# Message steps of six and five gather groups in turn, with 24 groups behind the last step

## The chip, the cores and the metric

The kernel runs on one core of one Trainium2 chip. The metric is the device time of one execution in microseconds. The kernel before took 2603.88 us, the median of 3 runs (2602.32 to 2604.92).

The engines are called TensorE (PE in the profile; PEld is its weight load, PEldq its sequencer's own instructions), VectorE (DVE), ScalarE (ACT), GpSimd (POOL) and SyncE (SP).

## The reference

`x` has 12500 rows (nodes) of 256 floats. `src` and `dst` name 200000 edges, sorted by `dst`; low node numbers have many more edges than high ones. What is computed:

```python
xn  = layernorm(x)
agg = segment_sum(xn[src], dst) / max(count of edges per dst, 1)
gnn = relu(agg @ W_l.T + b_l + xn @ W_r.T) + xn
# linear attention over all 12500 rows, 8 heads of 32:
Q, K = elu(xn @ Wq) + 1, elu(xn @ Wk) + 1;   v = xn @ Wv
msg  = (Q @ sum(K v)) / (Q . sum(K) + eps);  msg = layernorm(msg @ Wm) * g1 + b1
msg  = layernorm(relu(concat(xn, msg) @ W1) @ W2) * g2 + b2
x = x + gnn + (xn + msg)
# then: layernorm of x, a score per row, the 6249 best rows go through a
# gelu MLP of width 1024, are scaled by their score and added to x
```

## The kernel before, in words

Rows are tiled in 98 blocks of 128, two blocks to a step, so there are `NSUP` = 49 steps. The phases follow each other:

1. Normalization. The normalized rows go to a table in HBM (`xtab`) as two fp16 halves, high and low part, 512 fp16 values a row.
2. Key steps (49): K, Q and v of two blocks, sums over all rows, and Q and the transposed rows written to HBM.
3. Message steps (49): attention message, its projection, a two-layer MLP, and the product with `W_r`. A step is `m_body` on TensorE, VectorE and ScalarE, and `m_io` on SyncE. Two steps are unrolled in a loop body, `s` being the parity and `j` the number of the pair.
4. Linear phase: means of the aggregate (ScalarE, L1422, its first instruction waits for `agg_done`), their product with `W_l` (L1722) and the stored product of `W_r`, which GpSimd loads again (`lin_raw`, L722).
5. Choice of the best rows, and their MLP.

Along phases 2 and 3 runs the aggregation. The edges are cut into `NG` = 392 groups of 512, each of 4 lists of 128. GpSimd takes them in order (L708): per list one indirect DMA gathers 128 rows of `xtab` into a ring of `RING` = 6 slots (group g in slot g % 6). Before the first gather of group g it waits until group g - 6 is used (`grp_used`), and each gather raises the arrival semaphore `rows_in[slot]` by 16. The last five lists are left out, so group 390 has three gathers and group 391 none.

VectorE makes for every group and every block of nodes that the group touches a one-hot matrix (`one_hot`, L880), in 4 buffers. TensorE's `seg` (L1540 and on) loops over the blocks of a group: it waits for the arrival semaphore, the one-hot and a zeroed PSUM bank, multiplies each list twice (high part L1550, low part and count L1552), and after the last block marks the group as used (L1561). When a block is complete, VectorE adds its sum to `agg` and zeroes the bank (`add_before`, L890 and L892).

The groups are written into the steps by hand. A key step has 2 (groups 0 to 97). A message step has 6 in steps 0 to 41 and 5 in steps 42 to 48; 7 follow behind the last step, between the leftovers of it (`m_hidden`, `l_product`, `m_mlp_out` on TensorE, `norm_stats` and `m_end` on VectorE). With six groups a step the slot is the place in the step, so all slots are numbers of the program text. After the last group VectorE calls `add_before` twice, then reads the counts and sets `agg_done`.

What sets the order of the work is this text: each engine takes its instructions in order, and semaphores tie them.

Of the kernel before, what the change touches and what calls it, by code (L numbers as in the profile page):

```python
# [9 lines left out]
ALU = mybir.AluOpType  # L10
# [3 lines left out]
P = 128  # L14
N, D, E = 12500, 256, 200000
# [5 lines left out]
TPG = 4  # L21
GE = TPG * P
KG, MG = 2, 6
NG = NSUP * (KG + MG)
RING = 6
TAIL = 7
MFULL = NSUP - TAIL
# [35 lines left out]
assert NSUP % GCH == 0 and 0 < LASTC < P and KG * 3 == RING and MG == RING and MFULL % 2 == 0  # L63
# [52 lines left out]
def build(nc, x, src, dst, W_l, b_l, W_r, Wq, Wk, Wv, Wm, W1, W2, g1, b1, g2, b2, wr, br, w1, fb1, w2, fb2, out):  # L116
# [13 lines left out]
    with ctx:  # L130
# [147 lines left out]
        ones_set = sem("ones_set")  # L278
# [4 lines left out]
        k_x_in = [sem(f"k_x_in{i}") for i in range(3)]  # L283
# [17 lines left out]
        m_x_in = [sem(f"m_x_in{i}") for i in range(2)]  # L301
# [44 lines left out]
        s_in_col = sem("s_in_col")  # L346
        s_lane = sem("s_lane")
        s_a = sem("s_a")
# [120 lines left out]
        def k_place(s, j, t):  # L469

            return KG * s + t, j

        def m_first(i):

            return KG * NSUP + MG * i - (max(0, i - MFULL) if isinstance(i, int) else 0)

        def m_groups(i):

            return MG - 1 if isinstance(i, int) and i >= MFULL else MG

        def place(g):

            return g % RING, g // RING

        def m_place(i, t):

            if isinstance(i, int):
                return place(m_first(i) + t)
            slot, use = place(KG * NSUP + t)
            return slot, use + i  # L490

        tail = list(range(NG - TAIL, NG))

# [24 lines left out]
        def _(e):  # L518
# [43 lines left out]
            for i in range(2):  # L562
                e.dma_start(kx[i], rows(x, 2 * i)).then_inc(k_x_in[i], 16)
# [6 lines left out]
            def k_io(i, s, j):  # L570
                if not (isinstance(i, int) and i >= NSUP - 2):
                    if past(i, 1):
                        e.wait_ge(k_xn, i)
                    e.dma_start(kx[(s + 2) % 3], rows(x, 2 * i + 4)).then_inc(k_x_in[(s + 2) % 3], 16)
# [11 lines left out]
            def m_load(i, s):  # L586
                e.dma_start(mx[s], rows(x, 2 * i)).then_inc(m_x_in[s], 16)
                e.dma_start(flat(mq[s]), turned(q_d, i)).then_inc(m_q_in[s], 16)
# [70 lines left out]
        def _(e):  # L659
# [38 lines left out]
            e.memset(gath[:, :, 2 * D:2 * D + 1], 1.0).then_inc(ones_set, 1)  # L698
# [66 lines left out]
        def _(e):  # L765
# [222 lines left out]
            def m_body(i, s, j):  # L988
                g0 = m_first(i)
                spans = seg_values(e, mybir.EngineType.DVE, g0, m_groups(i))  # L990
# [35 lines left out]
                for t in range(5, m_groups(i)):  # L1026
# [6 lines left out]
            for t, g in enumerate(tail):  # L1033
                seg(g, BA, *seg_values(e, mybir.EngineType.DVE, g, 1)[0])
# [16 lines left out]
            add_before()  # L1051
            k = e.snap(full)
            e.wait_ge(seg_added, k + 2)
# [149 lines left out]
            for c in range(NPCH):  # L1203
                k, b = c % 2, slice(c * PCH, (c + 1) * PCH)
                if c >= 2:
                    e.wait_ge(s_mm, c - 1)
                v.tensor_tensor(s_is[k], bcast(col16, PCH, NSEL), s_col[:, b].unsqueeze(2).to_broadcast([P, PCH, NSEL]),
                                ALU.is_equal).then_inc(s_in_col, 1)
                v.tensor_tensor(s_oh[k], bcast(iota16, PCH, P), s_pos[:, b].unsqueeze(2).to_broadcast([P, PCH, P]),
                                ALU.is_equal)  # L1210
                e.wait_ge(s_in_col, c + 1)
                v.tensor_tensor(s_pc[k][:, :, NSEL:2 * NSEL], s_is[k], blk16[:, b].unsqueeze(2).to_broadcast([P, PCH, NSEL]),
                                ALU.mult).then_inc(s_a, 1)
# [55 lines left out]
        def _(e):  # L1269
# [52 lines left out]
            e.wait_ge(k_x_in[0], 16)  # L1322
# [4 lines left out]
            def k_body(i, s, j):  # L1327
                more = not (isinstance(i, int) and i == NSUP - 1)
                s1 = (s + 1) % 3
                if more:  # L1330
                    e.wait_ge(k_x_in[s1], 16 * (j + (s + 1) // 3) + 16)
                    e.wait_ge(k_xT_ps, i + 1)
                    xn_of(kxn, kx[s1], i + 1, k_xn)
# [53 lines left out]
            def m_body(i, s, j):  # L1387
# [13 lines left out]
                e.wait_ge(m_x_in[s], 16 * j + 16)  # L1401
# [64 lines left out]
            for c in range(NPCH):  # L1466
                e.wait_ge(s_in_col, c + 1)
# [37 lines left out]
        def _(e):  # L1505
# [32 lines left out]
            def seg(slot, use, first, more, end):  # L1538

                padded = max(0, (use * RING + slot + 1) * TPG - (NG * TPG - GPAD)) if isinstance(use, int) else 0  # L1540
                landed = 16 * TPG * use + 16 * (TPG - min(TPG, padded))
# [17 lines left out]
                one = gath[:, TPG * slot, 2 * D:2 * D + 1]  # L1559
# [5 lines left out]
            e.wait_ge(ones_set, 1)  # L1565

            e.wait_ge(agg_zero, NBATCH)
# [18 lines left out]
            def k_body(i, s, j):  # L1586
# [14 lines left out]
                seg(*k_place(s, j, 0), *spans[0])  # L1601
# [10 lines left out]
                seg(*k_place(s, j, 1), *spans[1])  # L1612
# [37 lines left out]

            def m_body(i, s, j):
# [10 lines left out]
                g0 = m_first(i)  # L1662
                spans = seg_values(e, mybir.EngineType.PE, g0, 1)
                seg(*m_place(i, 0), *spans[0])
                if past(i, 1):
                    m_hidden(i - 1, 1 - s, j - 1 + s, 0)
                spans += seg_values(e, mybir.EngineType.PE, g0 + 1, m_groups(i) - 1)
                seg(*m_place(i, 1), *spans[1])
# [4 lines left out]
                seg(*m_place(i, 2), *spans[2])  # L1673
# [8 lines left out]
                seg(*m_place(i, 3), *spans[3])  # L1682
                if past(i, 1):
                    m_mlp_out(i - 1)
                seg(*m_place(i, 4), *spans[4])
                e.wait_ge(m_yn, i + 1)
                transposes(BB, myn).then_inc(m_yT_ps, 1)
                for k in range(5, m_groups(i)):
                    seg(*m_place(i, k), *spans[k])
            steps(e, m_body, MFULL, 2)  # L1690
            for i in range(MFULL, NSUP):
                m_body(i, i % 2, i // 2)

            i = NSUP - 1
            for k, g in enumerate(tail):
                seg(*place(g), *seg_values(e, mybir.EngineType.PE, g, 1)[0])
# [5 lines left out]
                if k == 2:  # L1702
                    m_mlp_out(i)

# [52 lines left out]
            for c in range(NPCH):  # L1757
                e.wait_ge(s_a, c + 1)
# [82 lines left out]
```

## Time and profile before

| | us |
|---|---|
| median of 3 runs | 2603.88 |
| profiled execution | 2605.66 |
| its span, first to last instruction | 2603.9 |
| TensorE matmul busy | 2193.5 (84%) |
| GpSimd busy | 1695.5 (65%) |
| VectorE busy | 1329.9 (51%) |
| ScalarE busy | 901.4 (35%) |

Shares of the chain that ended last: TensorE 45%, GpSimd 29%, issue 13%, VectorE 7%, DMA 5%. Its largest line is the gather L708 with 28%. Key steps lie between about 112 and 597 us, message steps between 597 and 2041 us, and the leftovers up to 2078 us.

A row of a wait table gives the engine and line that stood idle, what ended the idle time, the sum, the number of times and the longest. "issue" is time in which the engine waited for nothing that the profile shows. The ends of matmuls are modelled, so the time between two starts says more than the duration of one.

### The profile page before, as it was taken

To read this page: it belongs to the slowest core of one execution; us is meant where nothing else is said; L and a number is where in the kernel's file an instruction comes from. 1 tells how busy PE (TensorE), PEld (TensorE's weight loads), DVE (VectorE), ACT (ScalarE), POOL (GpSimd) and SP (SyncE) were. 2 spreads that over 40 slices of the span, in tenths; PEclk is the share of its full clock that TensorE was granted. 3 is DMA by queue.
4 is the path that set the end of the run, shared out by engine and by line. 5 is a ranking of instruction groups with operands and counts; after the bars stand their busy time and mean duration, and the time that the engine had idled before them with its cause. 6 is when DMAs were issued, how large, how long until landed. Compare 5 with 4: busy or idle time off the path is not lost.

```text
span 2603.9 us, 48868 instructions
## 1 busy us (share of the span) xinstructions
PE 2193.5 (84%) x13352; PEld 1818.9 (70%) x13353; DVE 1329.9 (51%) x3157; ACT 901.4 (35%) x1949; POOL 1695.5 (65%) x1817
## 2 busy tenths in 40 slices
PE   1399999997888888888888888988899799379998
PEld 0287777775667666666676666777677688279998
DVE  8644444443444344454444454455555599844444
ACT  8433333331222222222222222222222268344554
POOL 3577777777777777777777777777777411045553
PEclk7699999998898999999999999999999899589999
DMA  9766666654555555555555555555555489611111
GB/s 326 232 194 186 184 184 179 188 181 146 160 157 153 152 154 164 157 160 155 153 158 160 153 161 157 152 153 165 158 162 166 142 276 297 214 34 43 45 44 35
DMA packets 218373, 419.29 MB, mean 161 GB/s; under 512 B 40580, under 2 KB 107142, under 8 KB 218287
## 3 DMA queue, kind: packets, MB, share of 16 engines
q0 software_dynamic: 88352, 243.57, 33.0%
q1 hardware_dynamic: 129118, 173.95, 19.9%
q8 instruction: 34, 0.56, 0.1%
q10 hardware_dynamic: 816, 0.79, 0.1%
q14 instruction: 53, 0.43, 0.1%
HBM read 321.63 MB, written 96.52 MB: 161 GB/s over the span
## 4 chain that ended last, share of the span: by engine, by line
PE 45%; POOL 29%; issue 13%; DVE 7%; DMA 5%; ACT 1%; DVEq 1%; POOLq 0%; ACTq 0%
POOL gath_raw L708 28%; PE ps L1782 11%; PE ps L1629 6%; PE ps L1550 5%; PE ps L1552 4%; PE ps L1595 4%; DMA gath_raw<-xtab,srcI 3%; PE ps L1722 3%; PE ps L1639 3%; PE ps L1535 2%; PE ps L1677 2%; PE ps L1647 1%; DVE stats L784 1%; PE ps L1609 1%; DVE gath_raw L803 1%
## 5 line engine op out<-in xcount | busy, mean ns | idle before, releaser
L708 POOL DMA_INDIRECT gath_raw<-xtab,srcI x1563 | 1483.6, 949 | 476.5 <-issue 460.7
L1550 PE MATMUL ps<-gath_raw,onehot 128*128 128x256 f16 x1956 | 480.3, 283 | 202.8 <-DMA gath_raw<-xtab,srcI 107.6
L880 DVE SCALAR_TENSOR_TENSOR onehot<-ps,blkbase,dstF 128x512 f32 x489 | 353.9, 745 | 257.8 <-issue 154.5
L1552 PE MATMUL ps<-gath_raw,onehot 128*128 128x257 f16 x1956 | 481.5, 283 | 0.0
L1550 PEld LDWEIGHTS ps<-gath_raw,onehot 128*128 x1956 | 195.2, 100 | 292.9 <-issue 263.4
L1629 PE MATMUL ps<-work,w_s 128*128 128x256 f32 x1568 | 392.9, 407 | 2.2 <-issue 1.7
L1629 PEld LDWEIGHTS ps<-work,w_s 128*128 128x128 f32 x1568 | 311.7, 204 | 48.7 <-issue 2.7
L954 DVE BATCH_NORM_STATS2 stats<-ps 128x6 f32<-128x256 f32 x196 | 74.4, 421 | 449.2 <-PE ps L1677 444.6
L1782 PE MATMUL ps<-split_raw 128*128 128x256 f32 x2376 | 293.3, 285 | 1.7 <-DVE split_raw L1231 1.5
L1782 PEld LDWEIGHTS ps<-split_raw 128*128 128x128 f32 x2376 | 288.4, 193 | 2.4 <-issue 1.9
L1363 ACT ACTIVATE work<-ps 128x512 f32<-128x512 f32 x98 | 58.5, 597 | 496.8 <-PE ps L1629 496.8
L1552 PEld LDWEIGHTS ps<-gath_raw,onehot 128*128 x1956 | 197.2, 101 | 40.3
L1595 PE MATMUL ps<-wkv_s,work 128*128 128x256 f32 x784 | 183.1, 387 | 5.4 <-issue 4.7
L1639 PE MATMUL ps<-w_s,work 128*128 128x256 f32 x784 | 182.3, 385 | 0.0
L1595 PEld LDWEIGHTS ps<-wkv_s,work 128*128 128x128 f32 x784 | 146.1, 191 | 25.3 <-issue 5.4
L1639 PEld LDWEIGHTS ps<-w_s,work 128*128 128x128 f32 x784 | 144.9, 190 | 18.5
L1398 ACT ACTIVATE work<-ps,b_s,g_s 128x256 f32<-128x256 f32 x98 | 49.9, 560 | 247.3 <-PE ps L1535 247.3
L1368 ACT ACTIVATE small<-small 128x2 f32<-128x2 f32 x98 | 19.9, 203 | 329.6 <-DVE small L962 329.6
L1495 ACT ACTIVATE agg<-ps,fb_s 128x256 f32<-128x256 f32 x200 | 83.9, 470 | 138.4 <-PE ps L1782 138.4
L1535 PE MATMUL ps<-ident,work 128*128 128x128 f32 x784 | 124.6, 282 | 5.6 <-ACT work L1422 5.6
L722 POOL DMA_DIRECT2D lin_raw<-lin_d x49 | 26.0, 532 | 124.6 <-PE ps L1722 109.0
L1535 PEld LDWEIGHTS ps<-ident,work 128*128 128x128 f32 x784 | 91.1, 142 | 17.8 <-ACT work L1422 5.7
(223 smaller groups left out, 2989.9 us busy)
## 6 DMA issues: line engine op xcount, KB each, us to landing
work<-x_in SPq DMA_DIRECT2D x98, 256.0 KB, 3.2
lin_raw<-lin_d POOLq DMA_DIRECT2D x49, 512.0 KB, 4.4
gath_raw<-xtab,srcI POOLq DMA_INDIRECT x1563
agg<-x_in SPq DMA_DIRECT2D x14, 896.0 KB, 7.4
xt_d<-work SPq DMA_DIRECT2D x49, 256.0 KB
q_d<-work SPq DMA_DIRECT2D x49, 256.0 KB, 2.7
work<-q_d SPq DMA_DIRECT2D x49, 256.0 KB, 3.4
work<-xt_d SPq DMA_DIRECT2D x49, 256.0 KB, 3.1
```

Of the source, the lines that this page charges most:

```text
L708: e.indirect_dma_start(out=gath[:, TPG * s + t, 0:2 * D], out_offset=None, in_=xtab[:, :], in_offset=bass.IndirectOffsetOnAxis(ap=srcI[:, ...
L880: v.scalar_tensor_tensor(out=onehots[:, ds(p % OHN * TPG, TPG), :], in0=ps[:, columns:columns + 1, 0:P].to_broadcast(shape), scalar=blkbas ...
L954: last = v.bn_stats(ln_st[k][:, u, :], src[:, u, :])
L1495: last = a.activation(fh[:, c, :], bank(BB + h)[:, c % 2, :], ACT.Gelu_apprx_tanh, bias=fb1_s[:, c:c + 1])
L1535: last = t.transpose(bank(b)[:, c, u * P:(u + 1) * P], of[:, u, c * P:(c + 1) * P], ident[:, :])
L1550: t.matmul(ps[:, ds(BG + k % 2, 1), 0:D], oh, gath[:, r, 0:D], start=False, stop=False, skip_group_check=True)
L1552: last = t.matmul(ps[:, ds(BG + k % 2, 1), 0:AGW], oh, gath[:, r, D:2 * D + 1], start=False, stop=q == TPG - 1, skip_group_check=True)
L1595: last = t.matmul(bank(BC + b)[:, u, :], kxT[s][:, c, u * P:(u + 1) * P], wkv_s[:, c, b * D:(b + 1) * D], start=c == 0, stop=c == 1)
L1629: last = t.matmul(bank(BD + h)[:, o_ % 2, :], w1_s[:, c, o_ * P:(o_ + 1) * P], (mxT[s] if c < 2 else mynT)[:, c % 2, :], start=c == 0, sto ...
L1639: last = t.matmul(bank(BF)[:, u, :], mh1[:, c, u * P:(u + 1) * P], w2_s[:, c, :], start=c == 0, stop=c == 3)
L1722: last = t.matmul(to[:, u, :], gaT[i % 2][:, c, u * P:(u + 1) * P], wlT[:, c, :], start=False, stop=c == 1, skip_group_check=True)
L1782: last = t.matmul(to, left[l], right[r], start=start and k == 0, stop=stop and k == 2)
```

## The change

- Message steps have 6 groups where the step number is even and 5 where it is odd, in all 49 steps, and all of them run in the loop of pairs. That makes 270 groups. The remaining 24 follow the last step: the first six between its leftovers, the others in loops of six.
- A pair has 11 groups, so a place in the pair meets another slot each time. `seg` on TensorE takes the slot as a register value in the message steps, and its gather operand's row is computed from it.
- Arrival semaphores: `landing(g)` names the semaphore for group g. Within the message steps places 6 to 10 of a pair have five new ones (`rows_m`), everything else uses `rows_in[g % RING]`. GpSimd calls it with its g; TensorE's `m_seg` calls it with the group of the first pair at that place and adds `TPG * j` lists to the count.
- The group mark takes its operand from slot 0.
- After the last group VectorE adds the block before last ahead of the wait for the last mark, and the last block behind it, without zeroing a bank.
- Some semaphores are merged: `x_rows_in` for the loads of x in both kinds of steps, `agg_zero` for the ones of the ring, `s_placed` in the choice of rows.

```diff
-KG, MG = 2, 6
-NG = NSUP * (KG + MG)
+KG = 2
+MPAIR = (6, 5)
+NG = NSUP * 8
 RING = 6
-TAIL = 7
-MFULL = NSUP - TAIL
+MAT = KG * NSUP
+TAILAT = MAT + sum(MPAIR[i % 2] for i in range(NSUP))
+TAIL = NG - TAILAT
...
+        rows_m = [sem(f"rows_m{i}") for i in range(sum(MPAIR) - RING)]
...
+        def m_first(s, j):
+            return MAT + sum(MPAIR) * j + sum(MPAIR[:s])
+
+        def landing(g):
+            p = (g - MAT) % sum(MPAIR)
+            return rows_m[p - RING] if MAT <= g < TAILAT and p >= RING else rows_in[g % RING]
+
+        def landed(g):
+            return TPG * len([o for o in range(g + 1) if landing(o) is landing(g)])
...
-                    ).then_inc(rows_in[s], 16)
+                    ).then_inc(landing(g), 16)
...
-            e.wait_ge(grp_used, NG)
             add_before()
-            e.reg_mov(before, held)
-            e.reg_mov(since, pair)
-            add_before()
-            k = e.snap(full)
-            e.wait_ge(seg_added, k + 2)
+            e.wait_ge(grp_used, NG)
+            b, k = e.snap(held), e.snap(full)
+            v.tensor_tensor(agg[:, ds(b, 1), :], agg[:, ds(b, 1), :], ps[:, ds(BG + k % 2, 1), 0:AGW], ALU.add).then_inc(sum_read, 1)
+            e.wait_ge(sum_read, k + 1)
...
-            def seg(slot, use, first, more, end):
+            def seg(rows_of, lists, slot, first, more, end):
...
+                row = slot * TPG if isinstance(slot, int) else e.snap(slot * TPG)
+                landed_at = 16 * lists
...
-                    e.wait_ge(rows_in[slot], landed)
+                    e.wait_ge(rows_of, landed_at)
...
-                        r = TPG * slot + q
+                        r = row + q if isinstance(row, int) else ds(row + q, 1)
...
+            def m_seg(s, j, t, span):
+                g = m_first(s, 0) + t
+                seg(landing(g), landed(g) + TPG * j, (m_first(s, j) + t) % RING, *span)
...
-            steps(e, m_body, MFULL, 2)
-            for i in range(MFULL, NSUP):
-                m_body(i, i % 2, i // 2)
+            steps(e, m_body, NSUP, 2)
...
+            with e.Fori(1, TAIL // RING - 1) as j:
+                spans = seg_values(e, mybir.EngineType.PE, TAILAT + RING * j, RING)
+                for k in range(RING):
+                    seg(landing(TAILAT + k), landed(TAILAT + k) + TPG * j, (TAILAT + k) % RING, *spans[k])
```

## Rows read from the trace of the kernel before

**Rows 1.** The page's first line.
```profile
span 2603.9 us, 48868 instructions
```

**Rows 2.** GpSimd's waits, 130 to 2060 us: us in total, times, longest us.
```profile
POOL gath_raw L708 <- issue: 452.8, 1486, 0.3
POOL gath_raw L708 <- PE ps L1561: 15.5, 51, 0.3
```

**Rows 3.** Line L708, 900 to 1900 us: ns min/median/max, first and last start.
```profile
L708 POOL DMA_INDIRECT gath_raw<-xtab,srcI x799: 942/946/1416, 899.6 to 1899.9; - x200
```

**Rows 4.** Timeline of GpSimd, the last gather: start us, us, what, idle before.
```profile
2055.22 0.95 POOL L708 DMA_INDIRECT gath_raw<-xtab,srcI  x1 [0.30 <-issue]
```

**Rows 5.** Chain of waits, 2070 to 2080 us: start us, us, what.
```profile
2070.14 1.58 issue
2071.72 0.39 PE ps L1550
...
2073.61 0.11 PE ps L1561
...
2074.60 0.43 DVE agg L890
...
2076.36 0.43 DVE agg L890
...
2076.82 0.44 DVE ps L892
...
2078.36 0.92 ACT work L1422 x2
```

**Rows 6.** Stretches, line L1550 alone: length, PE busy (x), PEld (x), clock, DMA, GB/s.
```profile
597.00:1858.00 1261.00, 323.68 (x1296) 130.79 (x1296) 0.94 0.52 156
1858.00:2041.00 183.00, 48.42 (x209) 20.28 (x209) 1.00 0.54 162
```

**Rows 7.** Timeline of TensorE, step 46: its start, five marks, the next step.
```profile
1962.82 1.14 PE L1659 MATMUL ps<-kvk,work 128*128 128x132 f32 x8 [1.16 <-issue]
...
1966.76 0.16 PE L1561 MATMUL ps<-gath_raw 128*1 128x1 f16 x1
...
1971.60 0.16 PE L1561 MATMUL ps<-gath_raw 128*1 128x1 f16 x1
...
1977.55 0.16 PE L1561 MATMUL ps<-gath_raw 128*1 128x1 f16 x1
...
1982.18 0.16 PE L1561 MATMUL ps<-gath_raw 128*1 128x1 f16 x1
...
1986.81 0.16 PE L1561 MATMUL ps<-gath_raw 128*1 128x1 f16 x1
...
1988.72 1.14 PE L1659 MATMUL ps<-kvk,work 128*128 128x132 f32 x8 [1.16 <-issue]
```

**Rows 8.** Timeline of TensorE, fifth and sixth mark of step 36.
```profile
1702.53 0.16 PE L1561 MATMUL ps<-gath_raw 128*1 128x1 f16 x1
...
1704.93 0.16 PE L1561 MATMUL ps<-gath_raw 128*1 128x1 f16 x1
```

**Rows 9.** Chain of waits, 284 to 292 us; the first is a group's last gather.
```profile
286.02 2.97 DMA gath_raw<-xtab,srcI
288.99 0.52 issue
...
289.79 0.11 PE ps L1552
...
290.56 0.09 PE ps L1561
```

**Rows 10.** Chain of waits, 745 to 765 us: both halves of the hidden layer.
```profile
748.02 4.86 PE ps L1629 x16
...
754.20 3.65 PE ps L1629 x16
```

**Rows 11.** Line L1550, 1858 to 2041 us: register operations of TensorE's sequencer.
```profile
L1550 PEldq FUSED_REGOPS  x265: 46/46/143, 1859.3 to 2040.7; - x133
```

More of the change, by code:

```diff
@@ L282, in build @@
         bnd_tab = sem("bnd_tab")
-        k_x_in = [sem(f"k_x_in{i}") for i in range(3)]
+        x_rows_in = [sem(f"x_rows_in{i}") for i in range(3)]
         k_xn = sem("k_xn")
@@ L562, in _ @@
             for i in range(2):
-                e.dma_start(kx[i], rows(x, 2 * i)).then_inc(k_x_in[i], 16)
+                e.dma_start(kx[i], rows(x, 2 * i)).then_inc(x_rows_in[i], 16)
             e.wait_ge(bnd_out, 16)
@@ L573, in k_io @@
                         e.wait_ge(k_xn, i)
-                    e.dma_start(kx[(s + 2) % 3], rows(x, 2 * i + 4)).then_inc(k_x_in[(s + 2) % 3], 16)
+                    e.dma_start(kx[(s + 2) % 3], rows(x, 2 * i + 4)).then_inc(x_rows_in[(s + 2) % 3], 16)
                 e.wait_ge(k_xnT, i + 1)
@@ L586, in m_load @@
             def m_load(i, s):
-                e.dma_start(mx[s], rows(x, 2 * i)).then_inc(m_x_in[s], 16)
+                e.dma_start(mx[s], rows(x, 2 * i)).then_inc(x_rows_in[s], 16)
                 e.dma_start(flat(mq[s]), turned(q_d, i)).then_inc(m_q_in[s], 16)
@@ L1025, in m_body @@
                     l_even(i - 1, 1 - s, j - 1 + s)
-                for t in range(5, m_groups(i)):
+                for t in range(5, MPAIR[s]):
                     seg(g0 + t, BA, *spans[t])
-            steps(e, m_body, MFULL, 2)
-            for i in range(MFULL, NSUP):
-                m_body(i, i % 2, i // 2)
+            steps(e, m_body, NSUP, 2)
             last_two = [(i, own_m + 10 * NSUP - 10 + 5 * k) for k, i in enumerate((NSUP - 2, NSUP - 1))]
-            for t, g in enumerate(tail):
-                seg(g, BA, *seg_values(e, mybir.EngineType.DVE, g, 1)[0])
+            for t in range(RING):
+                seg(TAILAT + t, BA, *seg_values(e, mybir.EngineType.DVE, TAILAT + t, 1)[0])
                 if t in (0, 5):
@@ L1045, in _ @@
                     m_end(i, i % 2, ch + 3)
-            e.wait_ge(grp_used, NG)
-            add_before()
-            e.reg_mov(before, held)
-            e.reg_mov(since, pair)
-            add_before()
-            k = e.snap(full)
-            e.wait_ge(seg_added, k + 2)
+            with e.Fori(1, TAIL // RING) as j:
+                g0 = TAILAT + RING * j
+                spans = seg_values(e, mybir.EngineType.DVE, g0, RING)
+                for t in range(RING):
+                    seg(g0 + t, BA, *spans[t])
+            add_before()
+            e.wait_ge(grp_used, NG)
+            b, k = e.snap(held), e.snap(full)
+            v.tensor_tensor(agg[:, ds(b, 1), :], agg[:, ds(b, 1), :], ps[:, ds(BG + k % 2, 1), 0:AGW], ALU.add).then_inc(sum_read, 1)
+            e.wait_ge(sum_read, k + 1)
             base = own_m + 10 * NSUP
@@ L1400, in m_body @@
                 last.then_inc(m_ynT, 1)
-                e.wait_ge(m_x_in[s], 16 * j + 16)
+                e.wait_ge(x_rows_in[s], 16 * (len(range(s, NSUP, 3)) + j + 1))
                 if past(i, 2):
@@ L1466, in _ @@
             for c in range(NPCH):
-                e.wait_ge(s_in_col, c + 1)
+                e.wait_ge(s_placed, 2 * c + 1)
                 if c >= 2:
@@ L1558, in seg @@
                 e.reg_alu(full, behind, 0, op=ALU.max)
-                one = gath[:, TPG * slot, 2 * D:2 * D + 1]
+                one = gath[:, 0, 2 * D:2 * D + 1]
                 k = e.snap(full)
@@ L1600, in k_body @@
                 spans = seg_values(e, mybir.EngineType.PE, KG * i, KG)
-                seg(*k_place(s, j, 0), *spans[0])
+                seg(rows_in[KG * s + 0], TPG * (j + 1), KG * s + 0, *spans[0])
                 if more:
@@ L1611, in k_body @@
                 last.then_inc(k_q_ps, 1)
-                seg(*k_place(s, j, 1), *spans[1])
+                seg(rows_in[KG * s + 1], TPG * (j + 1), KG * s + 1, *spans[1])
             steps(e, k_body, NSUP, 3)
@@ L1681, in m_body @@
                     l_product(i - 1, 1 - s)
-                seg(*m_place(i, 3), *spans[3])
+                m_seg(s, j, 3, spans[3])
                 if past(i, 1):
                     m_mlp_out(i - 1)
-                seg(*m_place(i, 4), *spans[4])
+                m_seg(s, j, 4, spans[4])
                 e.wait_ge(m_yn, i + 1)
                 transposes(BB, myn).then_inc(m_yT_ps, 1)
[L1688 to L1692, printed above, removed]
+                for k in range(5, MPAIR[s]):
+                    m_seg(s, j, k, spans[k])
+            steps(e, m_body, NSUP, 2)
             i = NSUP - 1
-            for k, g in enumerate(tail):
-                seg(*place(g), *seg_values(e, mybir.EngineType.PE, g, 1)[0])
+            for k in range(RING):
+                seg(landing(TAILAT + k), landed(TAILAT + k), (TAILAT + k) % RING, *seg_values(e, mybir.EngineType.PE, TAILAT + k, 1)[0])
                 if k < 2:
@@ L1703, in _ @@
                     m_mlp_out(i)
+            with e.Fori(1, TAIL // RING - 1) as j:
+                spans = seg_values(e, mybir.EngineType.PE, TAILAT + RING * j, RING)
+                for k in range(RING):
+                    seg(landing(TAILAT + k), landed(TAILAT + k) + TPG * j, (TAILAT + k) % RING, *spans[k])
+            spans = seg_values(e, mybir.EngineType.PE, NG - RING, RING)
+            for k in range(RING):
+                missing = min(TPG, max(0, TPG * (k + 1) - (TPG * RING - GPAD)))
+                seg(landing(NG - RING + k), landed(NG - RING + k) - missing, (TAILAT + k) % RING, *spans[k])
             def g_turn(i):
```

54 lines of the change are left out of this document (17 added, 37 removed).

## The prediction, made before the result was known

> **What bounds the kernel now.** I read the span first, then GpSimd's waits, because its gathers (L708) head the chain. From 130 to 2060 us GpSimd never idled longer than 0.3 us before a gather, whoever released it [rows 2]. It issues one gather per 1.25 us: 799 start between 899.6 and 1899.9 us, so (1899.9 - 899.6) / 798 = 1.2535, and 1.25 in stretches without a 1416 ns one [rows 3]. A group of four takes 5.01 us. So the 392 groups are bound by GpSimd's issue, and the last gather starts at 2055.22 us [rows 4]. Nothing TensorE does better can move that; what can move it is a slot that comes free late.
>
> The second view is TensorE over the message steps. The gap from the last gather's start to the first use of the means, at 2078.36, is 23.14 us [rows 4, 5]: TensorE is several groups behind at the end. A step of five groups that waits for no gather takes 1988.72 - 1962.82 = 25.90 us with 7 one-hot blocks [rows 7], against 25.03 us of gathers, so the last seven steps lose ground. After its last group mark a five-group step needs 1.91 us to the next step [rows 7]; a sixth group, one block, comes 2.40 us after the fifth mark [rows 8] and about 0.13 more ends the step: 25.90 - 1.91 + 2.53 = 26.52 us.
>
> **The new order of steps.** 49 steps hold 25 x 6 + 24 x 5 = 270 groups, and 24 follow. A pair of steps costs TensorE 25.90 + 26.52 = 52.42 us at 7 + 8 blocks. Blocks are fp16 matmuls of L1550 over four: 1296 / 4 = 324 in 252 groups early, 209 / 4 = 52 in 35 groups late [rows 6], so 14.1 and 16.4 per 11 groups. At 8 starts 0.11 us apart [rows 9], 0.88 us each, the pair is 51.6 and 53.7 us. GpSimd needs 44 x 1.2515 = 55.06. By this alone GpSimd stays the bound and TensorE arrives at the tail hardly behind. The tail's 24 groups take 120 us of gathers, far more than TensorE's leftovers of the last step (about 13 us of matmuls) plus some 2 us a group.
>
> **The end of the aggregation, shorter.** Now only the two last groups stand behind the last gather (group 391 has none). A seg starts 2.97 + 0.52 = 3.49 us after the last gather of its group starts [rows 9]. In a tail half idle I expect the lower clock level, as at the end of this one, where a block with its mark takes 2073.72 - 2071.72 = 2.0 us [rows 5], against 290.65 - 289.51 = 1.14 in the stretch of rows 9; two, with 0.5 between (bounds 0.1 and the 1.58 of a row in which the bounds are loaded between), give 3.49 + 2.0 + 0.5 + 2.0 = 8.0. From mark to sum is 2074.60 - 2073.72 = 0.9; then 2078.36 - 2076.36 = 2.0, less 0.45 for the zeroing no longer there [rows 5]. In all 10.4 us against 23.14: 12.7 saved, between 11 and 15 (full clock). The second add now costs nothing, since its first half stands ahead of the wait. The lin loads of GpSimd, which today wait for the last store behind the last gather, start at once, but were not the last wait before either. What is late next is the landing of the last gather. The phases behind begin as before and shift whole.
>
> **The waits, a cost that the title hides.** The scatter matmuls wait on landing(g). GpSimd evaluates it with the real g: for the first six places of a pair that is rows_in[g % 6]. TensorE evaluates it with the g of the first pair plus TPG * j. A pair has 11 groups, and 11 mod 6 is 5, so in pair j the semaphore on which place p waits is the one that the group at place (p + j) mod 6 increments. The five other places are exact. Hence, at j mod 6 = 1, place 4 has waited for place 5's group; at 2, place 0 waits for place 2's; and so on; at j mod 6 = 5, place 0 waits until the group five later has landed. Each gather of that group may start, as slots are free up to it; the next group's may not, since its slot is the one place 0 holds. At j mod 6 = 0 all is exact. Where the place waited for is an earlier one nothing is held.
>
> For j mod 6 from 1 to 4 this only makes TensorE trail by one to four groups; it has the slots for it. At j = 5, 11, 17, 23 GpSimd stops. With S the start of the last gather of the group waited for, the next gather was due at S + 1.25; place 0's mark ends at 290.65 - 286.02 = 4.63 after S [rows 9], so it stands 3.4 us, up to 3.7 with the issue gap of 0.3 [rows 2]. Then, marks in a step that waits for no gather: 4.84, 10.79, 15.42, 20.05 us after the first [rows 7], against 5.01, 10.01, 15.02, 20.02: the third is 0.8 late. So 4.3 us per event at full clock. But TensorE has just idled 5 us or more; after such gaps the 16 matmuls of L1629 took 4.86 us in place of 3.65 [rows 10], and a block 2.0 in place of 1.14: +0.9 and +1.2 or twice that. That makes 6.4 to 7.6. At j mod 6 = 4 (places 0 and 1 wait for places 4 and 5) the third mark comes at S + 4.63 + 10.79 = 15.4 against 1.25 + 15.02 = 16.3 due: nothing at full clock, 1 to 3 us at half clock or with a two-block first group. Per round of six pairs 4.3 to 11 us; I take 7, nearest to the half-clock rows. Four rounds: 28 us, between 17 and 44. TensorE regains 1.4 to 3.4 us of lag per pair between events, which is why the stop comes again in full each time: every j mod 6 = 5 demands five groups of lag exactly.
>
> The Trainium skill (DMA: Bandwidth & Descriptors, Anatomy of one DMA, SWDGE path) fits a GpSimd DMA of 128 KB at 2.0 + 0.3 = 2.3 us. The trace has 2.97 from the instruction's start, 2.02 from its end. Were 2.3 counted from the end, each stop and the last landing would be 0.3 longer: 1 us more in the sum.
>
> **Registers for the slot.** Gather slices in the message steps get their row from a register. Per block the sequencer runs 265 / 52 = 5 fused register operations of 46 ns [rows 6, 11], and matmuls start 0.11 us apart all the same [rows 9]. Cost bounds: nothing, or one more for each of 8 matmuls, 0.37 us x 14.1 = 5.2 us a pair, making 51.6 into 56.8, 1.8 over GpSimd, x 24.5 pairs = 43 us. I take nothing, the nearer row: the array works off 0.22 us per one-hot quarter, and one operation more hides there. The remainder by six, once per group, is hidden the same way, up to a few tenths after a wait.
>
> The merged semaphores (x_rows_in, agg_zero, s_placed) keep each wait at the same event: nothing, either way, as no instruction is added. Fewer unrolled steps: nothing seen, below 1 us.
>
> **Sum.** The profiled execution is 2605.66 us (span 2603.9 [rows 1] plus 1.8 around it). 2605.66 - 12.7 + 28 = 2621; its own time stood 1.8 above the median of the three runs, so 2619.
>
> **Rivals.** First, the other side: the later-place waits never stop GpSimd, because TensorE is that late anyway or the count is satisfied by other arrivals; then only the end gains: 2603.9 - 12.7 = 2591. It would decide if TensorE trailed five groups without being asked; against it stands that today it waits for gathers, that is, it trails by one group. Chance 0.17. Second, register arithmetic makes TensorE the bound: 2591 + 43 = 2634, and with part of the stops on top, 2634 to 2650. For it: a sequencer that must do twice as much between matmuls; against: the unchanged matmul spacing. 0.13. Third, the change does not do what it says but cheaply: stops at full clock and no more, 17 us, cancel the end's gain: 2591 + 17 = 2608, no measurable change. For it: clock 0.94 in the message steps [rows 6], so mostly full. 0.12. The forecast, 2619, own range 2609 to 2634, has 0.58.
>
> The range reaches from the first rival to the second's upper part: 2590 to 2647. Something like 0.2% (5 us) is what a measurement tells from no change: faster 0.18, same 0.11, slower 0.71.
>
> **What would show it.** GpSimd's waits: today's longest before a gather is 0.3 us; I expect four stops of 3.4 us or more near groups 159, 225, 291 and 357, with shorter ones up to 2 groups around, and 28 us in sum. TensorE's waits for gathers at place 0 of the six-group steps should be 5 us and more for j mod 6 = 1 to 5 and absent at 0. The last gather should start near 2083 us, and 10 us later the first use of the means. The step pairs should run at 55 us. Matmul spacing in L1550's group should stay 0.11; if it grows, the second rival. If the last gather still starts at 2055, the first rival is right and my reading of landing is wrong.

## The result, and the profile after

The changed kernel takes 2747.2 us (2745.89 to 2754.93, five runs) against 2603.88 us (2602.32 to 2606.46) for the kernel before: ratio 1.0557, 95% interval 1.0542 to 1.0572. That is 143 us slower, where 15 us were predicted; it lies outside the range. In 13 of the 18 runs of the next section the kernel before took 3062 to 3096 us instead of 2604 to 2606, for a cause that was not found; they are called the 3080 us runs below, the others the 2604 us runs, and every ratio is taken within one of the two groups.

First the page of the changed kernel: the span, then busy time and share of each engine.

```profile
span 2750.5 us, 51654 instructions
...
PE 2267.9 (82%) x13352; PEld 1837.3 (67%) x13353; DVE 1331.1 (48%) x3156; ACT 901.9 (33%) x1949; POOL 1696.1 (62%) x1817
```

The span stands against 2603.9 in [rows 1]. GpSimd's busy time is what it was (1695.5), TensorE's grew by 74 us. GpSimd's waits before a gather come next (us in total, times, longest us, 130 to 2210 us); they answer to [rows 2]:

```profile
POOL gath_raw L696 <- issue: 437.5, 1409, 1.4
POOL gath_raw L696 <- PE ps L1551: 187.8, 125, 8.1
```

The second line is the result in one row. GpSimd's wait for a free slot (the mark of TensorE, L1551) was 15.5 us with none above 0.3; now it is 187.8 us with a longest of 8.1. GpSimd no longer bounds the message steps. The last gather shows the sum (timeline: start, us, what, idle before); it answers to [rows 4], 2055.22:

```profile
2212.93 0.95 POOL L696 DMA_INDIRECT gath_raw<-xtab,srcI  x1 [0.30 <-issue]
```

So the gathers end 157.7 us later. The end of the aggregation, in the chain of waits (start, us, what), answers to [rows 5]:

```profile
2209.18 2.75 DMA gath_raw<-xtab,srcI
2211.93 0.52 issue
2212.45 0.39 PE ps L1540
...
2216.14 0.27 issue
2216.41 0.39 PE ps L1540
...
2219.18 0.12 PE ps L1551
...
2219.99 0.44 DVE agg L1042
...
2221.53 0.92 ACT work L1412 x2
```

From the last gather's start to the first use of the means it is 2221.53 - 2212.93 = 8.6 us instead of 23.14: 14.5 us less. And 157.7 - 14.5 = 143.2 us, all but 3.4 of the 146.6 us between the two spans. The gain at the end came about as predicted; the loss is in the message steps.

### The profile page after: what moved, and what is told of

It reads as the page before. It is cut to its first block, busy times and chain, and to the rows that moved or that the text cites. A ratio compares the mean times of both kernels' runs of the same rounds, so it can differ in the third digit from the quotient of the medians.

```text
span 2750.5 us, 51654 instructions
## 1 busy us (share of the span) xinstructions
PE 2267.9 (82%) x13352; PEld 1837.3 (67%) x13353; DVE 1331.1 (48%) x3156; ACT 901.9 (33%) x1949; POOL 1696.1 (62%) x1817
## 4 chain that ended last, share of the span: by engine, by line
PE 60%; issue 13%; POOL 10%; DVE 9%; DVEq 4%; DMA 3%; ACT 1%; POOLq 0%; ACTq 0%; SPq 0%
PE ps L1618 13%; PE ps L1782 10%; POOL gath_raw L696 9%; PE ps L1540 8%; PE ps L1542 6%; PE ps L1584 4%; PE ps L1628 4%; PE ps L1671 3%; PE ps L1722 3%; DVEq L463 2%; PE ps L1525 2%; DMA gath_raw<-xtab,srcI 2%; PE ps L1636 2%; DVE onehot L868 1%; PE ps L1551 1%
## 5 line engine op out<-in xcount | busy, mean ns | idle before, releaser
L1540 PE MATMUL ps<-gath_raw,onehot 128*128 (+1 forms) x1956 | 505.4, 288 | 236.7 <-DVE onehot L868 126.8
L868 DVE SCALAR_TENSOR_TENSOR onehot<-ps,blkbase,dstF 128x512 f32 x489 | 355.4, 746 | 439.6 <-issue 373.4
L1542 PE MATMUL ps<-gath_raw,onehot 128*128 (+1 forms) x1956 | 510.3, 290 | 0.0
L1540 PEld LDWEIGHTS ps<-gath_raw,onehot 128*128 x1956 | 194.4, 99 | 352.9 <-issue 290.0
L1618 PE MATMUL ps<-work,w_s 128*128 128x256 f32 x1568 | 403.6, 415 | 6.2 <-issue 4.5
L1618 PEld LDWEIGHTS ps<-work,w_s 128*128 128x128 f32 x1568 | 319.2, 209 | 57.9 <-issue 6.8
L1551 PEld LDWEIGHTS ps<-gath_raw 128*1 128x1 f16 x392 | 31.0, 79 | 118.9 <-issue 118.9
```

Source lines behind the costliest of these rows:

```text
L868: v.scalar_tensor_tensor(out=onehots[:, ds(p % OHN * TPG, TPG), :], in0=ps[:, columns:columns + 1, 0:P].to_broadcast(shape), scalar=blkbas ...
L1540: t.matmul(ps[:, ds(BG + k % 2, 1), 0:D], oh, gath[:, r, 0:D], start=False, stop=False, skip_group_check=True)
L1542: last = t.matmul(ps[:, ds(BG + k % 2, 1), 0:AGW], oh, gath[:, r, D:2 * D + 1], start=False, stop=q == TPG - 1, skip_group_check=True)
L1618: last = t.matmul(bank(BD + h)[:, o_ % 2, :], w1_s[:, c, o_ * P:(o_ + 1) * P], (mxT[s] if c < 2 else mynT)[:, c % 2, :], start=c == 0, sto ...
```

## The experiments

My theory after the first look was that three things add up: later-place waits of `landing`, register rows in `seg`, and VectorE's late start after the jump back of its loop. The rivals: the plan of six and five groups costs by itself; or one of the three carries everything.

**Exact waits (e1).** One table of the changed kernel altered, so that a place in an even step waits for the semaphore of the slot that it reads:

```diff
-            return rows_m[p - RING] if MAT <= g < TAILAT and p >= RING else rows_in[g % RING]
+            if MAT <= g < TAILAT:
+                return rows_m[p - RING] if p >= RING else rows_in[(MAT + p) % RING]
+            return rows_in[g % RING]
```

> The kernel after, with GpSimd raising for the first six places of a pair the semaphore on which TensorE waits for that place, so every wait is for the group's own lists. Theory A (waits for a later place stop GpSimd and leave it without lead): GpSimd's stops vanish, the last gather starts near 2055 us and the time is 2591, at most 2620. Theory B (register rows make TensorE's sequencer slow, 1.5 us of sequencer time a block in place of 0.5): TensorE is the bound from about pair 4 on whatever the waits are, and the time stays within 15 us of 2747. Theory C (VectorE's jump back at the end of a pair and its load of block numbers, 11 us with no one-hot, 1886.3 to 1897.5 us) says the same as B here.

> The kernel of e1_exact again (the kernel after with every wait for the group's own lists), on a chip on which the kernel before takes its usual 2604 us; on the first chip it took 3066, with gaps of 2 to 3 us between instructions of every engine that no semaphore explains. Theory A (later-place waits): 2591. Theories B (register rows) and C (VectorE's jump and load): within 15 us of 2747. On the slow chip it was 2.8% over the kernel before, which speaks for B and C.

> The changed kernel with one table altered: each of the six places of an even step waits for the arrival counter of the gather slot that it reads. Against the changed kernel's 2747 us, my theory, from the difference measured where all kernels were slower (0.8 to 1.1%): 22 to 30 us less, 2717 to 2725 us. Rival (the mismatched waits matter more where GpSimd has no stalls of its own, since its lead over TensorE is smaller there): 40 us or more less, under 2707 us. Rival (they matter less because register rows and the jump cover them): 2735 us or more.

> The changed kernel with exact waits at the six places of even steps. If the kernel before takes about 2604 us: 2717 to 2725 us by the difference of 0.8 to 1.1% found where all was slower; under 2707 us if the later-place waits matter more here; 2735 us or more if they are covered. If the kernel before takes about 3080 us: 1.025 to 1.032 of it again.

Measured: 1.0283, 1.0254 and 1.0315 of the kernel before in the 3080 us runs (the changed kernel itself: 1.0347, interval 1.0317 to 1.0377, below), and 2736.23 us, 1.0498 (1.0482 to 1.0515), in the 2604 us run. The changed kernel has 1.0557 (1.0542 to 1.0572). The waits take 0.59% of 2604, about 15 us (by the ends of the intervals 7 to 23), of the 143. The expectation of 22 to 30 us less was too high, and the main loss lies elsewhere.

**The changed kernel unchanged (a2)**, to have it in a 3080 us run:

> The kernel after, unchanged, in the setting of the other runs, in which the kernel before takes 3066 us instead of 2604 because the engines stand still for 2 to 3 us at regular places of their instruction streams (GpSimd once per 8 gathers). Against it e1_exact and e1b_exact (3153 and 3147) are to be held. Theory A (waits for later places): it is 30 to 140 us slower than e1, above 3175. Theories B (register rows) and C (VectorE's jump and load): within 15 us of e1. If the kernel before takes 2604 us here, the setting was the chip's, and this is 2747.

3201.7 us against 3092.52: 1.0347. That is 0.3 to 0.9% over the three of e1, by the ratios 10 to 29 us of 3092, and below the 30 to 140 that theory A expected.

**Register rows in the kernel before (e2).** The plan stays; the operand's row was meant to come from a register:

```diff
+                row = slot * TPG if at is None else e.snap(at * TPG)
...
-                        r = TPG * slot + q
+                        r = row + q if isinstance(row, int) else ds(row + q, 1)
```

> The kernel before, in which the gather operand's row in the message loop (steps 2 to 41) is computed from a register instead of a number of the text; slots, waits, steps and tail as before. Theory B: TensorE gets about 0.6 us per block and some tenths per group, 5 to 6 us a step, which eats the 3 to 5 us idle of a step of 30 us: 1 to 3 us over for 40 steps, 2640 to 2700. Theory A and C: 2604, within 5 us, since no wait and no jump is changed.

1.0004 (0.9976 to 1.0032), in a 3080 us run. But this run says nothing of register rows, because none reached the program. With six groups a step the slot is `(98 + 6 * i + t) % 6`, the same number for every step i. The traces agree: both kernels have 48868 instructions, and TensorE's sequencer does the same register operations at the first matmul of a quarter (whole execution; the kernel before, then e2):

```profile
L1550 PEldq FUSED_REGOPS  x2445: 46/46/162, 113.8 to 2072.0; - x189
L1551 PEldq FUSED_REGOPS  x2445: 3/46/711, 113.2 to 2529.0; - x189
```

The changed kernel has 2774 of them at that line and 987 plain ones besides. So e2 is a second timing of the kernel before, and what register rows cost in a kernel with room was not measured.

**Both engines written out (e4).** The new plan, but TensorE's and VectorE's 49 message steps are written out, with static rows and exact waits:

```diff
-                g = m_first(s, 0) + t
-                seg(landing(g), landed(g) + TPG * j, (m_first(s, j) + t) % RING, *span)
+                g = m_first(s, j) + t
+                seg(landing(g), landed(g), g % RING, *span)
...
-            steps(e, m_body, NSUP, 2)
+            for i in range(NSUP):
+                m_body(i, i % 2, i // 2)
```

> As the one before, with VectorE's message steps written out too: no jump back on it, block numbers still loaded once a step. All theories A, B and C: 2591, within 8 us. If it stays above 2620, none of the three holds what is left, and the load of block numbers (4 us on VectorE) or the fetch of instructions is next.

> The kernel of e4_both_flat again (6 and 5 in turn, 24 behind, TensorE's and VectorE's message steps written out), on a chip on which the kernel before takes 2604 us. All theories: 2591, within 8 us. On the slow chip it was 0.7% under the kernel before.

> The 6/5 plan with TensorE's and VectorE's message steps written out, static gather rows and exact arrivals for every place, timed beside a kernel before of about 2604 us. My theory (the changed plan is sound and the 143 us are later-place waits, register rows and VectorE's jump): GpSimd is the bound in the pairs again at 55 us each, and the end of the aggregation is some 12 to 14 us shorter, so 2588 to 2596 us. Rival (the plan of six and five groups itself costs in the pairs): 2604 us or more.

> The 6/5 plan with both engines' message steps written out, static gather rows and exact arrivals. If the kernel before takes about 2604 us beside it: 2588 to 2596 us by my theory (the end of the aggregation is 12 to 14 us shorter, nothing else changes, and GpSimd bounds the pairs), 2604 us or more by the rival that the plan itself costs in the pairs. If the kernel before takes about 3080 us: 0.993 to 0.997 of it again.

0.9932, 0.9936 and 0.9958 in the 3080 us runs; in the 2604 us run 2590.89 us against 2606.26, ratio 0.9943 (0.9928 to 0.9957). This is the only version faster than the kernel before, by 15 us. GpSimd's waits in it, 130 to 2060 us, are as in [rows 2]:

```profile
POOL gath_raw L696 <- issue: 455.3, 1494, 0.3
POOL gath_raw L696 <- PE ps L1552: 13.1, 43, 0.3
```

and its end, in the chain of waits:

```profile
2057.76 3.36 DMA gath_raw<-xtab,srcI
...
2067.80 1.72 ACT work L1413 x4
```

The last gather starts 2.5 us later than before, and 10.04 us behind it the means are used; the prediction had 10.4. So the first use of the means comes 10.6 us earlier than before; the rest of the 15 us lies behind it (1.9 us in the two traces) or between timings. The rival that the plan itself costs has fallen.

**The kernel before, written out (e8).** Is the gain of e4 due to the writing out?

```diff
-            steps(e, m_body, MFULL, 2)
-            for i in range(MFULL, NSUP):
+            for i in range(NSUP):
```

> The kernel before with its message steps 2 to 41 written out on TensorE and VectorE as well; six groups in them, five in the last seven, tail of seven, as before. It tells how much of e4's 0.65% comes from the order of steps and how much from the writing out. If the order does it (end of the aggregation 12.7 us shorter, as predicted): ratio 0.998 to 1.003 here. If the writing out does it: 0.991 to 0.996.

2606.14 against 2603.9 us, 1.0007 (0.9997 to 1.0016). No: in the old plan the loops cost nothing.

**Only TensorE written out (e3).** As e4, but VectorE keeps its loop, so this edit is in TensorE's program alone:

```diff
-            steps(e, m_body, NSUP, 2)
+            for i in range(NSUP):
+                m_body(i, i % 2, i // 2)
```

> The plan of the kernel after (6 and 5 groups in turn, 24 behind), but TensorE's message steps are written out 49 times, so its slots and arrival counts are numbers and every wait is for the group's own lists. VectorE keeps its loop of pairs. Theory A and B: 2591 (last gather at 2055 us, 10 us behind it the first mean). Theory C: VectorE's 11 us without a one-hot per pair still hold TensorE, which has 1.4 to 3.4 us a pair to spare: 4 to 7 us a pair late from the point where the ring is full, 2650 to 2700.

> Static rows, exact waits, TensorE written out, VectorE's steps 2 to 41 in the loop of the changed kernel. VectorE's jump costs some 88 us beside register rows (2736 against 2648 us). If it costs the same where TensorE has slack: about 2680 us. If, as I hold, TensorE's slack of 2 to 3 us a pair and the ring absorb most of what VectorE comes late: 2595 to 2640 us, since the kernel before jumps as often and has 2604. Where the kernel before takes about 3080 us: 1.006 to 1.012 of it.

1.0087 (1.0058 to 1.0116) and 1.0111 (1.0075 to 1.0148), both in 3080 us runs. The first, timed together with e4 (0.9932), is 1.6% above it, from VectorE's loop alone: neither the nothing of the first two theories nor all of the third. (VectorE's loop here is that of the changed kernel, steps 2 to 47.) There is no 2604 us run of it.

**Later-place waits on static rows (e5).** As e4, with the changed kernel's `landing(m_first(s, 0) + t)`:

```diff
+                g = m_first(s, 0) + t
+                seg(landing(g), landed(g) + TPG * j, (m_first(s, j) + t) % RING, *span)
```

> The kernel of e4_both_flat (message steps written out on TensorE and VectorE, rows from numbers of the text) with the arrival waits of the kernel after: place p of pair j waits for the group at place (p + j) mod 6. Alone this tells the price of the waits. The prediction's size: 28 us (17 to 44) over e4_both_flat, 3075 where that takes 3047, or 2619 against 2591 where the kernel before takes 2604. If GpSimd is itself slowed by stalls of its own and TensorE has more to spare, less, down to 10.

> As the first of this set, with the changed kernel's waits at the six places of even steps (the place p of pair j waits for the group at place (j+p) mod 6). The prediction's own sum for these waits was 28 us (17 to 44) where nothing else is changed: 2605 to 2635 us, likeliest 2619. Rival (they never stop TensorE): equal to the first of this set.

> Static rows, both engines' steps written out, and the changed kernel's waits at the six places of even steps. Where the kernel with exact waits is 2591 us: 28 us more by the prediction's own term (17 to 44), so 2608 to 2635, likeliest 2619; 2591 if the waits never stop TensorE when it is not late anyway; about 2606 if they cost what they cost inside the changed kernel (15 us). Where the kernel before takes about 3080 us: 1.001 to 1.005 of it.

1.0042 (1.002 to 1.0064), 1.0019 (1.0002 to 1.0036) and 1.0017 (0.9997 to 1.0037), all in 3080 us runs. Timed together with e4 the difference is 1.0019 - 0.9958 = 0.6%; against e4 at other times (0.9932 and 0.9936) up to 1.1%. As an estimate, these shares of 2604 us are 16 to 29 us. The trace shows the mechanism. The first gathers of groups 159, 225, 291 and 357 (timeline of GpSimd, the last run of the three):

```profile
1074.73 0.95 POOL L696 DMA_INDIRECT gath_raw<-xtab,srcI  x1 [5.47 <-PE ps L1552]
...
1484.23 0.95 POOL L696 DMA_INDIRECT gath_raw<-xtab,srcI  x1 [5.53 <-PE ps L1552]
...
1900.79 0.95 POOL L696 DMA_INDIRECT gath_raw<-xtab,srcI  x1 [5.45 <-PE ps L1552]
...
2309.59 0.95 POOL L696 DMA_INDIRECT gath_raw<-xtab,srcI  x1 [6.50 <-PE ps L1552]
```

Four stops, at the four groups that the prediction named, of 5.45 to 6.50 us: 5.2, 5.2, 5.1 and 6.2 beyond the usual 0.3. The 3080 us runs have other stops before gathers too, but at the same four groups e4 in such a run has 0, 0.8, 0 and 2.6: 18 us less in sum, near the 16 of the times.

**Register rows on the written-out steps (e6).** As e4, with the slot from a register that counts groups:

```diff
+            turn = e.alloc_register("pe_turn")
+            e.reg_mov(turn, MAT)
...
-                seg(landing(g), landed(g), g % RING, *span)
+                seg(landing(g), landed(g), e.snap(turn) % RING, *span)
+                e.reg_add(turn, turn, 1)
```

> The kernel of e4_both_flat (written out on TensorE and VectorE, own arrivals), with the gather operand's row of the message steps taken from a register again, by the same operations per block as in the kernel after. It splits the 1.7 to 1.9% that TensorE's loop of pairs and its register rows cost together (e1 against e3). Theory B (the sequencer's register work, 0.375 us per quarter block where the array needs 0.22, about 0.6 us a block, 8 us a pair of which 1.5 to 3 are spare): 1.0 to 1.8% over e4, ratio to the kernel before 1.004 to 1.012. Theory D (TensorE's jump at the end of a pair and the fetch behind it cost it): within 0.3% of e4, ratio 0.991 to 0.997.

2649.87 against 2603.9 us, 1.018 (1.0163 to 1.0197): against e4 (0.9943) 2.4%, 62 us, for nothing but where the row number comes from. That is above the 1.0 to 1.8% expected. Here are quarters of blocks in TensorE's timeline. The kernel with static rows, e4:

```profile
1604.65 0.27 PE L1543 MATMUL ps<-gath_raw,onehot 128*128 128x257 f16 x1
1604.76 0.27 PE L1541 MATMUL ps<-gath_raw,onehot 128*128 128x256 f16 x1
1604.87 0.27 PE L1543 MATMUL ps<-gath_raw,onehot 128*128 128x257 f16 x1
1604.98 0.27 PE L1541 MATMUL ps<-gath_raw,onehot 128*128 128x256 f16 x1
```

and e6:

```profile
1603.48 0.27 PE L1543 MATMUL ps<-gath_raw,onehot 128*128 x1
1603.59 0.27 PE L1541 MATMUL ps<-gath_raw,onehot 128*128 x1
1603.71 0.27 PE L1543 MATMUL ps<-gath_raw,onehot 128*128 x1
1603.99 0.28 PE L1541 MATMUL ps<-gath_raw,onehot 128*128 x1
1604.12 0.28 PE L1543 MATMUL ps<-gath_raw,onehot 128*128 x1
1604.36 0.27 PE L1541 MATMUL ps<-gath_raw,onehot 128*128 x1
1604.49 0.28 PE L1543 MATMUL ps<-gath_raw,onehot 128*128 x1
1604.74 0.27 PE L1541 MATMUL ps<-gath_raw,onehot 128*128 x1
```

Starts are 0.11 us apart throughout in e4. In e6 they are so for the first quarters, for which the sequencer was ahead; then a quarter takes 1604.36 - 1603.99 = 0.37 us, not 0.22: the array waits for the sequencer, whose register records grow at just these lines (counts below).

**VectorE written out in e1 (e9).** TensorE keeps the changed kernel's loop and register rows; the edit is in VectorE's program:

```diff
-            steps(e, m_body, NSUP, 2)
+            for i in range(NSUP):
+                m_body(i, i % 2, i // 2)
```

> The kernel of e1_exact with VectorE's message steps written out and TensorE's still in the loop with register rows. Theory C (VectorE's jump and the load behind it hold TensorE at the start of a pair): it takes back 1.0 to 1.6% from e1's 1.025 to 1.028, so 1.010 to 1.017. Theory B alone (register rows decide, VectorE's jump is beside them): within 0.4% of e1.

2648.27 us, 1.0169 (1.0152 to 1.0186). The same as e6, so TensorE's own jump adds nothing to its register rows. Against e1 (1.0498) it is 3.3% less, where 1.0 to 1.6% were expected: VectorE's loop takes 86 us. GpSimd's waits for a slot in the two kernels, first e1:

```profile
POOL gath_raw L698 <- PE ps L1553: 161.1, 108, 6.8
```

then e9:

```profile
POOL gath_raw L698 <- PE ps L1554: 76.2, 91, 4.8
```

84.9 us less. The step down to e4 (13.1) is another 63, and the step up to the changed kernel (187.8) is 27, where the times have 15; the waits of GpSimd are not a measure to the us.

**The ladder**, 2604 us runs, as ratios to the kernel before:

| kernel | ratio | step, us |
|---|---|---|
| new plan, written out, static rows (e4) | 0.9943 | -15 |
| and register rows in TensorE's loop (e9) | 1.0169 | +59 |
| and VectorE's loop (e1) | 1.0498 | +86 |
| and later-place waits (the changed kernel) | 1.0557 | +15 |

(Each step is the difference of two ratios times 2604; the kernels were not all timed together, hence 145 and not 143.) The steps are priced in this order only.

## Why the prediction was wrong

**The steps that failed** are two terms of the sum that were put at nothing: "I take nothing, the nearer row" for the registers, and "Fewer unrolled steps: nothing seen, below 1 us". They measured 59 to 62 us and 86 us. "By this alone GpSimd stays the bound", the pair of TensorE taken as 51.6 to 53.7 us against GpSimd's 55.06, holds for the plan alone: e4 has it with static rows and written-out steps, and gains 15 us. But this margin is 1.4 to 3.4 us per pair, and both costs fall on it.

**Registers for the slot: taken as nothing, is 59 to 62 us.** The upper bound in the prediction, one more register instruction per matmul and 43 us, was below the truth. For the lines of the two matmuls and 1000 to 1300 us the changed kernel has (count, ns min/median/max, first and last start):

```profile
L1540 PEldq FUSED_REGOPS  x391: 42/79/149, 1000.1 to 1297.8; - x196
...
L1540 PE MATMUL ps<-gath_raw,onehot x264: 269/273/421, 1001.7 to 1298.0; 128*128 x132
L1540 PEldq ALU_OP  x196: 32/32/32, 1000.2 to 1298.0; - x196
L1542 PEldq FUSED_REGOPS  x261: 46/51/51, 1000.3 to 1298.1; - x131
```

264 matmuls are 66 blocks: 5.9 fused operations and 3 plain ones per block at the first matmul and 4 fused ones at the second, where [rows 11] had 5 at the first, and the second (L1552 there) had none. So the upper bound counted rightly, some eight more a block; but half of the fused ones at L1540 now take 79 ns or more, not 46. My error was to compare a count of instructions with 0.22 us of array work and say that one more hides: a quarter now starts 0.37 us after the one before it. The second rival ("register arithmetic makes TensorE the bound", 0.13) had the right mechanism and named the right sign, matmul spacing; its 2634 to 2650 us covers what e6 and e9 measured, 2649.87 and 2648.27. That is partly luck, since its upper end had stops by later-place waits in it, and these two kernels have none.

**"Fewer unrolled steps: nothing seen, below 1 us": is 86 us.** It is the largest term, priced beside register rows. The chain of waits of the changed kernel at one jump of VectorE (start, us, what; DVEq is VectorE's sequencer, L80 the loop, L463 the load of block numbers, L868 the one-hot):

```profile
1886.34 0.07 DVEq L80
1886.41 3.85 issue
1890.26 0.10 DVEq L80
1890.36 2.61 issue
1892.97 4.06 DVEq L463
...
1897.49 0.76 DVE onehot L868
1898.25 0.59 issue
1898.84 0.39 PE ps L1540
```

From the branch to the one-hot 11.15 us pass, 3.85 + 2.61 of them without any instruction. TensorE stands meanwhile, and then GpSimd (timelines of the two, idle before and what ended it):

```profile
1898.84 0.39 PE L1540 MATMUL ps<-gath_raw,onehot 128*128 x1 [5.85 <-DVE onehot L868]
...
1901.68 0.94 POOL L696 DMA_INDIRECT gath_raw<-xtab,srcI  x1 [6.07 <-PE ps L1551]
```

It is so at all 22 jumps of the loop with a next pair: 6.0 to 7.9 us from the branch to the load, mean 6.8. In the kernel before the records of the same jump read (start us, us, line, instruction):

```
1671.10 0.072 L78  COMPARE_BRANCH
1671.44 0.105 L78  FUSED_REGOPS
1671.65 4.081 L463 TENSOR_LOAD
1676.18 0.750 L880 SCALAR_TENSOR_TENSOR (one-hot)
```

0.55 us to the load, and at 19 jumps much the same. So the load of about 4 us was in the trace of before, without harm there, and it stands in e4 and e9 too; the 6.3 us more between jump and load are new.

The trace says what they are: VectorE waits for its code. The DMA packets of kind "instruction", 697 to 1858 us, the kernel before and then the changed one (packets, MB, share), and in the changed one 1886 to 1895 us alone, around the jump above:

```profile
q14 instruction: 10, 0.08, 0.0%
...
q14 instruction: 102, 0.84, 0.2%
...
q14 instruction: 3, 0.02, 1.5%
```

A row does not name the engine that the code is for, but the times do. Three packets of 8 KB follow each of the 22 jumps within 9 us (here they start at 1888.05, 1890.99 and 1893.65 us), and behind the 19 jumps of the kernel before there is one in all. VectorE's first instruction of the next pair starts 1.8 to 2.2 us after the first packet does, the load 1.7 to 2.0 us after the second, at all 22. Why the loop of the changed kernel is read again at each turn and the old one is not, is not shown.

The trace of before could not tell of this. What it could have told is that my TensorE pair was read from step 46 [rows 7], which is written out and has no jump in it, and that the change leaves TensorE 2.6 us of room per pair (55.06 - 52.42) where six and six groups left it 7.0 (60.1 - 2 x 26.52). e3 shows that the jump costs with static rows too (1.6%, a 3080 us run).

**Later-place waits: 28 us predicted, 15 us inside the changed kernel, 16 to 29 on static rows.** The reading of `landing` holds and so do the groups at which GpSimd stops. The first rival (they never stop it) is refuted by e5. A stop is smaller than I had it, 5.1 to 6.2 us there and not 6.4 to 7.6. But in the changed kernel they are partly covered: in e1, where every wait is exact, GpSimd stands before place 6 in 18 of the 19 pairs from 5 to 23, for 1.2 to 6.5 us, because TensorE is late by registers and jump. The stop that I tied to every sixth pair comes in nearly each.

**The clock.** The granted clock over 597 to 1858 us is 0.92 in the changed kernel against 0.94 [rows 6]; it is 0.92 in e1 too, and 0.96 and 0.97 in e9 and e4, which have no jump of VectorE. Behind the stop shown above, 5.85 us idle, the next one-hot quarters start 0.4 us apart instead of 0.22, so part of the loss at each stop is this, as the prediction had it for its own stops. I have not separated it.

**The end of the aggregation: 12.7 us saved predicted (11 to 15), 14.5 measured,** and 13.1 in e4. The block of group 390 starts 3.48 us behind the last gather's start, as predicted (3.49). What was off is behind it: the last two blocks take 1.7 and 1.0 us with 0.1 between, where I had 2.0 and 2.0 with 0.5, since the quarters of the last block start 0.22 us apart and not 0.43. The fit of the Trainium skill (DMA: Bandwidth & Descriptors, Anatomy of one DMA) that the prediction weighed gives 2.3 us. The landing in the chain above is 2.75 us from the instruction's start and 1.8 from its end, that in e4's chain 3.36 and 2.4. The one lies between the two readings, the other beyond both, and they decide nothing.

**The signs named in advance** worked: a last gather far beyond 2083 us, pairs of 62.9 us on average instead of 55 (steps 8 to 46 start at 829.10 and 2024.90 us, 19 pairs), and a spacing above 0.11 in L1540's group (0.37 us a quarter, not 0.22). Each pointed away from the forecast, and the last at one of the two causes. The range failed since I let the rivals exclude each other, when all can act at once and share one margin.

## What to carry to other kernels

Before calling one engine the bound, divide the margin: here it was 55.06 - 52.4 us per pair, and three small costs stood in line for it. Take the price of a step from steps in the form that they will have after the change (in a loop, with register operands), not from written-out ones. And before a run without a difference is believed, look in its trace whether the edit is there: e2 had the same time because it was the same program, and e8 says only that the old loop's jump, 0.55 us to the load, costs nothing, not that the changed loop's would.

## What the runs showed of the hardware that was not expected

- The matmul pair of a one-hot quarter whose gather row comes from a register starts every 0.37 us (e6), with a static row every 0.22 (e4), with some eight more register operations a block ahead of it.
- One loop back-edge on VectorE costs 0.34 us to the next instruction in the kernel before and 3.5 to 5.5 in the changed one, with no more records in the body (187 to 237 per turn before, 164 to 230 in the changed kernel). The Trainium skill (Advanced Engine Details and Errata, Control Flow Timing) states about 108 ns for a compare-and-branch. The branch's own record is 66 to 75 ns in both, so what differs stands behind it: three packets of code of 8 KB, 2.4 to 3.3 us apart, which the changed kernel has at every turn.
- The load of block numbers takes 0.7 to 5.7 us on VectorE in the changed kernel (108 loads, median 1.6); right behind the 22 jumps it takes 1.6 or 4.1.
- In the 3080 us runs GpSimd's gathers halt for some 2.2 us about every eight gathers, and the profile names no partner within the core for a good part of it. GpSimd's waits of e5, last run, 130 to 2600 us:

```profile
POOL gath_raw L696 <- remote: 326.1, 126, 4.0
```

Its cause was not looked for; it hits the kernel before as well.
